# Two feed-forwards around causal attention on one core: probabilities turned by DMA transposes, the work listed by slots, and six first feed-forwards run ahead

## What is computed

```
x = x + 0.5 * ffn(layernorm(x), W_up, W_gate, W_down)      # 256 -> 1024 -> 256, silu(up) * gate
x = x + attn(layernorm(x), wq, wk, wv, wo)                 # 16 heads of 16, rotary, causal softmax
x = x + 0.5 * ffn(layernorm(x), W_up, W_gate, W_down)
# W_up, W_gate, W_down are each replaced by  clip(round(W / scale), -1, 1) * scale,  scale = mean(|W|)
```

## Time and profile before

| what | us |
|---|---|
| median of 3 runs | 887.43 (884.81 to 891.82) |
| the profiled execution | 886.57 |
| its span | 884.8 |
| first row maxima of the first pair | at 102.7 |
| row maxima of the last pair | at 846.1 |

### The profile page before, as it was taken

How to read it: one execution, slowest core, us unless ns; L and a number is a source line. 1 busy time by engine, 2 the same in 40 slices (tenths; PEclk the granted TensorE clock), 3 DMA queues, 4 the chain that set the end, 5 groups by cost and what they waited for, 6 DMA issues and landing times.

```text
span 884.8 us, 18797 instructions
## 1 busy us (share of the span) xinstructions
PE 708.4 (80%) x6976; PEld 584.6 (66%) x6976; DVE 709.8 (80%) x1591; ACT 620.1 (70%) x1365; POOL 557.4 (63%) x568
## 2 busy tenths in 40 slices
PE   0537578888888979898988888897979898767756
PEld 0325366777777868677777777786868777655544
DVE  2753486989998898988898999899898889777663
ACT  2104387878878788878887887878787788767642
POOL 2026685676768676767777676867676767744232
PEclk9968797999999999999999999999999999989798
DMA  8300312030303040302113030303040211213000
GB/s 317 119 1 1 72 29 45 13 66 9 73 13 73 14 72 13 72 14 48 39 21 65 1 73 14 72 14 73 14 72 14 55 31 31 55 29 57 1 13 13
DMA packets 110297, 40.20 MB, mean 45 GB/s; under 512 B 100992, under 2 KB 109440, under 8 KB 109696
## 3 DMA queue, kind: packets, MB, share of 16 engines
q1 hardware_dynamic: 109632, 36.71, 20.0%
q10 hardware_dynamic: 576, 2.29, 0.7%
HBM read 9.63 MB, written 4.19 MB: 16 GB/s over the span
## 4 chain that ended last, share of the span: by engine, by line
ACT 30%; PE 28%; DVE 19%; POOL 12%; issue 9%; DMA 1%; DVEq 0%; POOLq 0%; SPq 0%; ACTq 0%
PE misc_ps L386 7%; ACT prob L639 5%; ACT prob_h L630 5%; ACT tanh_b L648 5%; ACT prob L641 4%; PE pv_ps L435 4%; PE up_ps L386 3%; PE probt_ps L453 3%; POOL hid_l L1027 3%; DVE hid L934 3%; PE misc_ps L500 3%; ACT prob_t L634 3%; DVE silu_b L923 3%; PE score_ps L403 2%; POOL k_row L334 2%
## 5 line engine op out<-in xcount | busy, mean ns | idle before, releaser
L1027 POOL TENSOR_TENSOR hid_l<-hid,hid_h 128x512 f16<-128x512 f32 x128 | 148.5, 1161 | 225.9 <-ACT hid_h L654 210.9
L630 ACT ACTIVATE prob_h<-probt_ps 128x384 f16<-128x384 f32 x256 | 127.5, 498 | 76.5 <-PE probt_ps L453 76.2
L639 ACT ACTIVATE prob<-score_ps,exp_bias,exp_scale 128x256 f32<-128x256 f32 x256 | 147.2, 575 | 2.3 <-DVE exp_bias L874 1.2
L453 PE MATMUL probt_ps<-ident_f,prob 128*128 128x128 f32 x768 | 133.0, 283 | 13.8 <-ACT prob_t L634 13.8
L386 PE MATMUL up_ps<-xt_hi,tern_up 128*128 128x256 f16 x512 | 127.4, 286 | 20.2 <-DVE tern_up L708 13.1
L1020 POOL TENSOR_TENSOR prob_l<-prob_t,prob_h 128x384 f16<-128x384 f32 x128 | 118.1, 923 | 37.0 <-ACT prob_t L634 36.8
L386 PE MATMUL down_ps<-tern_down,hid_h 128*128 128x256 f16 x512 | 121.0, 276 | 19.3 <-POOL hid_l L1027 19.2
L386 PE MATMUL up_ps<-xt_lo,tern_up 128*128 128x256 f16 x512 | 127.4, 286 | 0.0
L386 PE MATMUL gate_ps<-xt_hi,tern_gate 128*128 128x256 f16 x512 | 123.9, 280 | 1.8 <-DVE tern_gate L708 1.8
L386 PE MATMUL gate_ps<-xt_lo,tern_gate 128*128 128x256 f16 x512 | 123.1, 279 | 0.0
L641 ACT ACTIVATE prob<-score_ps,exp_bias,exp_scale 128x128 f32<-128x128 f32 x256 | 121.2, 473 | 0.0
(11 more groups left out here) (101 smaller groups left out, 1868.4 us busy)
## 6 DMA issues: line engine op xcount, KB each, us to landing
xs<-x SPq DMA_DIRECT2D x16, 256.0 KB, 2.8
out<-xs SPq DMA_DIRECT2D x16, 256.0 KB, 2.1
raw_gate<-w_gate_t ACTq DMA_DIRECT2D x1, 1024.0 KB, 7.6
raw_up<-w_up_t SPq DMA_DIRECT2D x1, 1024.0 KB, 7.7
raw_down<-w_down_t SPq DMA_DIRECT2D x1, 1024.0 KB, 10.4
raw_w<-wqkvo ACTq DMA_DIRECT2D x1, 1024.0 KB, 12.5
cos<-rope_cos SPq DMA_DIRECT2D x1, 512.0 KB, 13.6
sin<-rope_sin SPq DMA_DIRECT2D x1, 512.0 KB, 14.4
```

Of the source, the lines that this page charges most:

```text
L453: mm = pe.transpose(probt_ps[:, n * P:(n + 1) * P], prob[:, pair % 2, j, col * P:(col + 1) * P], ident_f[:, :])
L630: act.activation(prob_h[:, pair % 2, j, :], probt_ps[:, 0:384], ACT.Copy).then_inc(prob_h_done, 1)
L639: act.activation(prob[:, s % 2, j, 0:256], score_ps[:, j, 0:256], ACT.Exp, bias=exp_bias[:, j:j + 1], scale=exp_scale[:, :])
L1027: pool.tensor_tensor(hid_l[:, s % 2, :, :].rearrange("p m n -> p (m n)"), hid[:, s % 2, :], hid_h[:, s % 2, :, :].rearrange("p m n -> p (m ...
```

## The change

It rewrites the order and parts of the attention:

- **Slots.** Steps give way to one list of slots, numbered from the first pair (slot n holds pair n). `PLAN` puts the feed-forward rounds on slots: the first feed-forwards of batches 0 to 5 from slot -15 on, that of batch b from 6 on at slots 8(b-6)+17 to +20, the second feed-forward of batch b at 8b+13 to +16. Slots without a round are 9 to 12 and, from 97 on, four of each eight. There is one order for each engine in every slot; the `_OTHER` and `_EXTRA` tables are gone.
- **Probabilities.** All six blocks of a pair are rounded by ACT in one copy of 768 columns, POOL makes their low part in one subtraction of 768, and SP turns both parts with one DMA transpose (`turn_probs`). `product_v` of pair n stands in slot n+3. The PE transposes, `probt_ps`, ACT's `prob_hi` and `prob_t` from PSUM and DVE's low part are gone.
- **Scores.** The two heads of a pair share the matmuls: one bank holds the second query tile of both heads, the other the first. The maxima are written to PSUM.
- **Rotation.** DVE multiplies by cos and sin straight from `misc_ps`; ACT's copy and POOL's two products are gone.
- **Output of a pair.** DVE scales from PSUM first and adds the two parts afterwards.
- **Buffers.** `up_ps` and `tanh_b` have two, `xt_hi1`/`xt_lo1` too.

```diff
-PE_SLOT = ["scores", "product_v", "misc_a", "transpose_0", "up", "gate", "transpose_1", "misc_b",
-           "down"]
-ACT_SLOT = ["misc_a", "prob_hi_0", "tanh", "exps_0", "prob_hi_1", "exps_1", "misc_b", "hidden_hi"]
-DVE_SLOT = ["row_max", "pv_inverse", "exp_biases", "pv_add", "misc_a", "pv_scale", "silu", "hidden",
-            "prob_lo_1", "misc_b"]
...
+PAIRS = NBATCH * SLOTS
+PV_LAG = 3
+FIRST_FFN = -15
+AHEAD = 6
...
+    plan = [(FIRST_FFN + ROUNDS * b + r, 1, b, r) for b in range(AHEAD) for r in range(ROUNDS)]
+    plan += [(SLOTS * (b - AHEAD) + 17 + r, 1, b, r) for b in range(AHEAD, NBATCH) for r in range(ROUNDS)]
+    plan += [(SLOTS * b + 13 + r, 2, b, r) for b in range(NBATCH) for r in range(ROUNDS)]
...
+OF_BATCH = [("norm2", -8, "b"), ("qk0", -7, "b"), ("qk1", -6, "a"), ("v", -5, "b"), ("attn_t", 10, "b"),
+            ("out_proj", 11, "a"), ("norm3", 12, "b")]
+MISC = sorted([(SLOTS * b + at, place, what, b) for what, at, place in OF_BATCH for b in range(NBATCH)] +
+              [(FFN_START[1, b] - 1, "a", "norm1", b) for b in range(NBATCH)])
...
+STATS_LEAD = {1: 2, 2: 2, 3: 1}
...
+ROPE_ADD = {-6: 0, -5: 1}
+ROPE_HI = {-5: 0, -4: 1}
+ROW_LO = {-4: 0, -3: 1}
...
+PE_SLOT = ["scores", "product_v", "misc_a", "up", "gate", "misc_b", "down"]
+ACT_SLOT = ["prob_hi", "misc_a", "tanh", "exps_0", "exps_1", "rope_hi", "misc_b", "hidden_hi"]
+DVE_SLOT = ["row_max", "exp_bias", "pv_inverse", "ffn_added", "pv_scale", "misc_a", "norm_stats", "pv_add", "silu",
+            "norm_mean", "hidden", "norm_var", "norm_apply", "misc_b"]
+POOL_SLOT = ["norm_power", "rope_add", "prob_lo", "row_lo", "norm_apply", "hidden_lo"]
...
+            def turn_probs(n):
+
+                sp.wait_ge(prob_l_done, n + 1)
+                if n >= 2:
+
+                    sp.wait_ge(pv_done, n - 1)
+                sp.dma_start_transpose(prob_t[:, n % 2, :, :, :].rearrange("p a c q -> p (a c) q"),
+                                       prob_hl[:, n % 2, :, :].rearrange("p a k -> p (a k)")
+                                       ).then_inc(prob_turned[n % 2], 16)
...
+                pe.wait_ge(exp_done[0], n)
+                second = score_ps[:, 0, :].rearrange("p (j n) -> p j n", j=2)
+                pe.matmul(second[:, :, P:2 * P], ident_b[:, :], mask_b[:, :].rearrange("p (j n) -> p j n", j=2),
+                          start=True, stop=False, skip_group_check=True)
+                pe.matmul(second, q[:, P:2 * P], k, start=False, stop=True, skip_group_check=True)
...
+                pe.wait_ge(prob_turned[n % 2], 16 * (n // 2 + 1))
...
+            def exps(n, tile):
+
+                act.wait_ge(bias_done, n + 1)
+                if tile and n >= 2:
+
+                    act.wait_ge(prob_l_done, n - 1)
...
+            def prob_hi(n):
+                act.wait_ge(exp_done[0], n + 1)
+                act.wait_ge(exp_done[1], n + 1)
+                if n >= 2:
+
+                    act.wait_ge(prob_turned[n % 2], 16 * (n // 2))
+                act.activation(prob_hl[:, n % 2, 0, :], prob[:, n % 2, :], ACT.Copy).then_inc(prob_h_done, 1)
...
+                    dve.tensor_tensor(rope_c[:, tile, :], misc_ps[:, :], cos[:, tile, :], ALU.mult)
+                    dve.tensor_tensor(rope_s[:, tile, :], misc_ps[:, :], sin[:, tile, :], ALU.mult
+                                      ).then_inc(misc_taken, 1)
...
+            def prob_lo(n):
+                pool.wait_ge(prob_h_done, n + 1)
+                pool.tensor_tensor(prob_hl[:, n % 2, 1, :], prob[:, n % 2, :], prob_hl[:, n % 2, 0, :], ALU.subtract
+                                   ).then_inc(prob_l_done, 1)
...
+            def slot(g):
+                for what in POOL_SLOT:
+                    if what == "norm_power":
+                        for k, b in STATS_AT.get(g, []):
+                            norm_power(k, b)
```

More of the change, by code:

```diff
@@ L103 @@
[L103 to L125, removed]
@@ L128, in misc_through @@
[L128 to L155, removed]
@@ new lines, in through, with added, pair_at, batch_event @@
+def through(what, b):
+    return MISC_INDEX[what, b] + 1
+def added(f, b):
+    return FFN_ORDER.index((f, b)) + 1
+def pair_at(slot):
+    return slot if 0 <= slot < PAIRS else None
+def batch_event(slot, table):
+    for at, value in table.items():
+        b, rest = divmod(slot - at, SLOTS)
+        if rest == 0 and 0 <= b < NBATCH:
+            return b, value
+    return None
+def run_slots(engine_slot, before={}):
+    for g in range(FIRST_SLOT, LAST_SLOT + 1):
+        if g in before:
+            before[g]()
+        engine_slot(g)
@@ new lines, in misc @@
+                mm.then_inc(misc_written, 1)
+            def slot(g):
+                for what in PE_SLOT:
+                    if what == "scores" and pair_at(g) is not None:
+                        scores(g)
+                    elif what == "product_v" and pair_at(g - PV_LAG) is not None:
+                        product_v(g - PV_LAG)
+                    elif what.startswith("misc"):
+                        for name, b in MISC_AT.get((g, what[-1]), []):
+                            misc(name, b)
+                    elif what == "up" and g in ROUND_AT:
+                        up(*ROUND_AT[g])
+                    elif what == "gate" and g in ROUND_AT:
+                        gate(*ROUND_AT[g])
+                    elif what == "down" and g - 1 in ROUND_AT:
+                        down(*ROUND_AT[g - 1])
@@ L560, in _ @@
             pe.wait_ge(ident_loaded, 16)
-            run_steps(pe, step, before={1: lambda: pe.wait_ge(casts_done, 3)})
+            run_slots(slot, before={0: lambda: pe.wait_ge(casts_done, 3)})
         @block.scalar
@@ new lines, in _, with slot @@
+            of_round = {"silu": silu, "hidden": hidden}
+            of_norm = {"norm_stats": norm_stats, "norm_mean": norm_mean, "norm_var": norm_var}
+            def slot(g):
+                for what in DVE_SLOT:
+                    if what in of_pair:
+                        part, lag = of_pair[what]
+                        if pair_at(g - lag) is not None:
+                            part(g - lag)
+                    elif what in of_round and g in ROUND_AT:
+                        of_round[what](ROUND_AT[g][0])
+                    elif what in of_norm:
+                        for k, b in STATS_AT.get(g, []):
+                            of_norm[what](k, b)
+                    elif what == "norm_apply":
+                        for k, b in STATS_AT.get(g - 1, []):
+                            if k == 3:
+                                norm_apply(k, b)
+                    elif what == "ffn_added" and g in FFN_ADD:
+                        ffn_added(*FFN_ADD[g])
+                    elif what.startswith("misc"):
+                        for name, b in MISC_AT.get((g, what[-1]), []):
+                            misc(name, b)
```

760 lines of the change are left out of this document (301 added, 459 removed), and 6 rows, old and new, of the table ACT_OTHER.

## The result

The changed kernel takes **916.14 us** in the median of four runs (912.86 to 916.91), against 887.93 for the kernel before beside it: ratio 1.0308, 95% interval 1.026 to 1.0357. It is slower. The forecast was 872, and 916 lies 2 us above the range's upper end. The profiled execution took 912.9, its span is 911.0.

What follows compares the result with a forecast made beforehand. No single engine bounds the kernel, but a loop over engines with POOL's queue order late: 105 head, 65, 493 (full steps of 49.3) and 166 for slots, 41 tail sum to 870, plus 1.8 gives 872 us; range 816 to 914.

Steps and rivals of the forecast that it cites:

- the clock's term: Slots 7 and 0 of a step: PE's near-idle stretch drops it to 1.2 GHz, 1.0 us a step.
- The slots by themselves: The eight slots of a full step, worked out singly from 4.0 to 8.1 us, sum 48.3.
- the slots outside the full steps: Slots 0 to 12 at 5.0 each, 65 us; slots 93 to 126 at 4.8 with a round, 5.0 without, 166.
- The head: Before the first pair: set-up, four rounds, 11 slots of about 3.3 us, 8 for norms on POOL: 105 us.
- The tail: After the last pair: prob_hi, prob_lo and DMA (6.4) replace old transposes and copies (4.5): 41 us.
- DVE's work in a step: DVE in a full step: about 42 us of work against 43 before, almost nothing saved.
- rival 2: POOL's hold-up is absorbed, the step falls to 44.5, 824 us reported (808 to 848); chance 0.22.
- rival 1: The forecast: POOL's queue order stops PE about 3.5 us a step in slots 7 and 0, 872 us; chance 0.45.
- Rival 3: PE's clock falls with less work, +3.3 us a step, 913 us; decides under mean clock 0.88; chance 0.20.
- Rival 4: DMA transposes come late in slots 4 and 5, product_v stops PE 2 to 3 us a step, 900; chance 0.08.
- Rival 5: On DVE, bias and scaling stretch as before, 0.6 us a slot where DVE decides, 902 us; chance 0.05.
- The count: Slots with both pair and round fall from 116 to 108, ten full steps among them; the gain was placed here.

Runs made afterwards that it cites:

- fill: Changed kernel plus matmuls that compute nothing where TensorE waits (before norm 3's and norm 1's transposes and slot 7's down): 881.17 us, ratio 0.994.
- best: Changed kernel reordered: norm 1 a slot earlier, ACT's v copy first, DVE's mean and variance before silu, POOL's powers behind prob_lo, norm 3 applied where POOL idles: 804.56 us.
- power_late: Changed kernel with only POOL's list changed, the norm powers of a slot last instead of first: 879.88 us, ratio 0.9926.
- turn_twice: Changed kernel with every pair's DMA transpose issued a second time into an unread tile, which the copy into prob_hl also awaits: 947.05 us, ratio 1.0674.
- dummy_turns: Changed kernel with six float32 PE transposes a pair of the identity put back where the old ones stood: 911.77 us, ratio 1.0262.
- bias_sbuf: Changed kernel with the negated maxima written to SBUF again instead of PSUM: 942.11 us, ratio 1.0605.

## Why the prediction was wrong

**The step that failed: the clock's term.** I took 1.0 us a step for half clock, behind one stretch of TensorE in slots 7 and 0, from four microseconds at 1.2 GHz. `fill` measured 3.8. Behind that pause it was 1.3 to 1.4. The rest, 2.4, stands behind the pause before norm 3 in slot 4: I had it in the sum as a long slot, and its half clock at nothing, though the earlier trace rows is just that case. The slots by themselves were close: I summed them to 48.3, with the clock filled they take 47.4, and each is within 0.5 of my figure (in the order 5, 6, 7, 0 to 4: 4.0 and 3.96; 5.5 and 5.2; 5.6 and 5.9; 7.2 and 7.1; 4.7 and 4.6; 6.0 and 5.9; 7.2 and 7.1; 8.1 and 7.6). 2.8 us a step too little is 28 us, and my slots, 0.9 too long, give back 9; 17 us were measured for slots 13 to 92, since the first two steps are shorter (49.6 and 50.7).

**The second: the slots outside the full steps.** Slots 0 to 12 took 5.65 each instead of 5.0, together 8.5 us more: slots 3 and 4 take 7.8 and 7.7, and slot 12, norm 3's, 7.5 with a pause of 5.6 us and half clock behind it. Slots 93 to 126 gave 6.5 more: those with a round took 4.7, about as summed, those without 5.5 instead of 5.0, and norm 3's, with the same pause, 7.5. The head gave 5.6 more; where norm 1's work stands a slot earlier the head falls to 101.2. The tail gave 3.7; the clock is 0.72 in it, where it was 0.89 in the tail of the kernel before.

**One term was off without deciding.** I had DVE's work in a step at 42 us; the middle's busy time comes to 37.5 a step of 51.2. So rival 2's step of 44.5 was no floor either: `best` takes 42.3 to 42.9.

**POOL's order** (rival 1) was right as a mechanism, to 0.1 us on `xhat`, and its price was larger than I gave: the pause before `down` comes from it (`power_late` takes it from 3.2 to 0.9) and brings half clock. The pause before norm 3 is more than POOL's order: it is the place of norm 3 in DVE's list, behind `silu` and `hidden`, and its two passes, which take 2.06 us beside POOL's instructions instead of 0.73. With both pauses gone the same work takes 804.56 us.

**Rival 3, the clock,** came true: 913 was its time and 0.88 its limit; measured 916 and 0.87. That its time fits is in part luck, since the head and the slots outside the full steps gave 24 us where it had 8. Its cause was not the one named ahead of it, TensorE's amount of work. `best` has the same work in a step at 1.00, and in the changed kernel the half clock stands behind the pauses. I had both a pause of 3.5 us and the row that shows what follows one, and priced the second at a quarter of what two pauses cost.

**Rival 4** fell for the full steps (`turn_twice`). **Rival 5** fell: `exp_bias` takes 222 ns throughout. But I put the part's worth at 0.25 us a slot where DVE decides; undone it costs 26 us, done alone in the kernel before it brings 15.

**The count** of slots with pair and round was little gain in itself: the changed kernel at full clock (881) is only 8 us below the kernel before. `best`, at the same clock and with the same parts, is 77 us below `fill`, some 5 of which are the added matmuls in the tail: the orders of the queues held back more than the clock did.

What stays open: how long or how empty a stretch must be for the clock to fall. Pauses of 3.2 and 4.5 us were followed by half clock in every full step of the changed kernel from 230 us on (one of 3.0 at 198 was not), those of 1.8 and 1.5 in `best` between 200 and 600 us in one step of nine, those of 2.4 and 3.5 in `dummy_turns` in most. Behind slot 93 of `best`, after slots without a round, a pause of 1.6 was followed by half clock three times (clock 0.98 from 620 to 631 us, 0.50 from 631 to 636). The middle of the kernel before was not given such a pause.

## What to carry to other kernels

Price every pause of TensorE, not one of them, with what comes behind it: here 7.7 us of waiting in a step cost 3.8 more at half clock, so a queue's order that makes such a pause costs half as much again. Before an instruction that waits is put at the head of a queue, list all that stands behind it and who waits for that; moving one of two norms that met on one queue a slot ahead was worth 53 us. Where a change rewrites both the parts and their order, try the order by itself: seven lines of order took this kernel from 3% slower than before to 9.5% faster.

## What the runs showed of the hardware

- A `tensor_scalar` of VectorE that reads and writes SBUF alone waits for GpSimd's instruction even when it is tiny: 4 columns took 1.55 us beside `prob_hl` (`bias_sbuf`), `var_s` of 2 columns 1.17 (in `best`, 426.67 to 427.84, with POOL's `prob_hl` until 427.81), and a pass of `xhat` 0.41 alone or up to 1.86. With its input in PSUM the same bias took 221 to 224 ns 128 times. The Trainium skill ("SBUF — State Buffer", section "Who interferes with whom") counts `tensor_scalar` among the operations that can take the port pair shared with GpSimd, and says that the later one then blocks for the other's whole instruction. By that rule, the trace agrees, to 0.02 and 0.03 us.
- Not every VectorE instruction from SBUF to SBUF waits: the 96 norm statistics (L727, 256 columns) took 403 to 430 ns throughout in `best`.
- With the DMA transposes doubled and a DMA share of 0.91, the full steps stayed at 51.2 us; at a share of 0.97, in the shorter steps behind slot 93, TensorE waited up to 2.7 us for a transpose.
